# A graph convolution with sorted edges: the second stream's sums are stored as plain blocks of 127 or 255 rows, and the place columns are multiplied in bf16

## The reference, cut to what matters

```python
def _rgcn_edge_conv(h, xe, src, dst, etype, w, rt, b):
    m = jax.nn.relu(h[src] + xe)
    seg = etype * n + dst
    sums = jax.ops.segment_sum(m, seg, num_segments=R * n)
    cnt = jax.ops.segment_sum(jnp.ones((m.shape[0],), m.dtype), seg, num_segments=R * n)
    mean = sums / jnp.maximum(cnt, 1.0)[:, None]
    out = jnp.einsum('rnd,rdo->no', mean.reshape(R, n, -1), w)
    return out + h @ rt + b
...
h = jnp.maximum(_layernorm(x, axis=-1), 0.0)
for l in range(L):
    h = _rgcn_edge_conv(h, xe, src, dst, edge_type, weight[l], root[l], bias[l])
    h = _batch_norm(h, bn_gamma[l], bn_beta[l])
    if l != L - 1:
        h = jax.nn.relu(h)
return x + h
```

## Time and profile before

| | |
|---|---|
| median of 3 runs | 2361.72 us (2359.91 to 2362.99) |
| profiled execution | 2347.37 us, span 2345.3 us |
| mean granted TensorE clock | 0.912 |
| PE busy | 1950.2 us, 83% |
| PE weight load busy | 1623.0 us, 69% |
| DVE busy | 1434.1 us, 61% |
| ACT busy | 1193.5 us, 51% |
| POOL busy | 1443.9 us, 62% |

### The profile page before, as it was taken

The page is one execution under the profiler, slowest core; times in us unless marked ns, Lnnn a source line. Parts: engine busy times, 40 slices in busy tenths (PEclk is TensorE's granted clock), DMA queues, the critical chain, the costliest instruction groups (busy, mean ns, idle before and its releaser), DMA issues. The chain is left out here.

```text
span 2345.3 us, 58410 instructions
## 1 busy us (share of the span) xinstructions
PE 1950.2 (83%) x22268; PEld 1623.0 (69%) x22268; DVE 1434.1 (61%) x4328; ACT 1193.5 (51%) x2472; POOL 1443.9 (62%) x1377
## 2 busy tenths in 40 slices
PE   2499999999998889799788887787778787769866
PEld 1288888888777767799676675666556566659855
DVE  8766777777776565488765554444444444528554
ACT  0166777877776665344244443343333343424565
POOL 6746777777777775200377777777777777741000
PEclk8599999999999999899898999988998889979966
DMA  8724555555554553799633333333323333259799
GB/s 325 304 83 130 148 158 162 157 153 157 148 152 137 155 159 92 283 418 417 222 111 110 110 107 96 97 93 98 89 83 97 88 99 90 68 198 329 243 416 402
DMA packets 260695, 409.54 MB, mean 175 GB/s; under 512 B 38627, under 2 KB 170334, under 8 KB 260412
## 3 DMA queue, kind: packets, MB, share of 16 engines
q1 hardware_dynamic: 192566, 225.92, 29.2%
q0 software_dynamic: 46192, 99.84, 14.7%
q10 hardware_dynamic: 21654, 79.99, 8.4%
HBM read 255.41 MB, written 150.19 MB: 173 GB/s over the span
## 5 line engine op out<-in xcount | busy, mean ns | idle before, releaser
L853 POOL DMA_INDIRECT acc<-arena x550 | 583.9, 1062 | 223.6 <-issue 160.6
L1775 PE MATMUL ps_o<-arena 128*128 128x128 f32 x3152 | 458.9, 306 | 217.8 <-DVE arena L1224 215.2
L1775 PEld LDWEIGHTS ps_o<-arena 128*128 128x128 f32 x3152 | 420.8, 215 | 305.6 <-DVE arena L1224 298.5
L838 POOL DMA_INDIRECT arena<-h_rows,arena x394 | 438.9, 1114 | 301.0 <-DMA h_rows<-chunk_mem 181.2
L838 POOL DMA_INDIRECT arena<-in_x_dram,arena x394 | 403.4, 1024 | 125.5 <-issue 119.7
L1706 PE MATMUL ps_t<-arena 128*128 128x256 f32 x1576 | 453.2, 411 | 12.1 <-DVE arena L1198 8.1
L1198 DVE TENSOR_SCALAR arena<-arena 128x256 f32<-128x256 f32 x788 | 273.9, 410 | 128.3 <-PE ps_o L1725 128.1
L1184 DVE TENSOR_TENSOR arena<-arena,bn_b 128x512 f32<-128x512 f32 (+1 forms) x99 | 69.7, 704 | 448.7 <-DMA arena<-h_rows,arena 448.7
L1706 PEld LDWEIGHTS ps_t<-arena 128*128 128x128 f32 x1576 | 274.7, 194 | 96.2 <-issue 69.5
L1511 ACT ACTIVATE arena<-ps_o 1x512 f32<-1x512 f32 (+1 forms) x196 | 113.2, 577 | 423.7 <-PE ps_o L1775 423.6
L1480 ACT ACTIVATE arena<-ps_t 128x512 f32<-128x512 f32 x396 | 233.2, 589 | 179.7 <-PE ps_t L1706 179.5
(11 more groups left out here) (281 smaller groups left out, 2399.8 us busy)
## 6 DMA issues: line engine op xcount, KB each, us to landing
arena<-in_edge_attr_dram SPq DMA_DIRECT2D x190, 256.0 KB
chunk_mem<-acc SPq DMA_DIRECT2D x55, 512.0 KB, 8.4
acc<-arena ACTq DMA_DIRECT2D x28, 896.0 KB, 24.0
arena<-in_x_dram SPq DMA_DIRECT2D x45, 512.0 KB, 9.7
arena<-acc SPq DMA_DIRECT2D x43, 512.0 KB, 12.4
chunk_mem<-hn_rows SPq DMA_DIRECT2D x41, 512.0 KB, 12.7
out_dram<-arena ACTq DMA_DIRECT2D x38, 512.0 KB, 9.0
acc<-arena SPq DMA_DIRECT2D x238, 56.0 KB
```

Of the source, the lines that this page charges most:

```text
L838: pool.indirect_dma_start(out=hb[:, hb_slot(gg), t // NG, :], out_offset=None, in_=(x, h1_tab)[l], in_offset=at(src_t[:, t:t + 1])).then_i ...
L853: pool.indirect_dma_start(out=acc[l], out_offset=at(idx_t[:, t:t + 1]), in_=ob[:, gg % OB, t // NG, :], in_offset=None, **how).then_inc(co ...
L1775: last = te.matmul(ps_sum[:, c], sm[:, gg % SM, b, j, :], yb[:, gg % 2, b, j, :], start=b == 0, stop=b == NH - 1)
```

## The change

Four things change together.

1. **Blocks.** All of stream 1 (tiles 100 to 194) goes out as plain blocks: 127 rows for the first 31 tiles, 255 rows for the other 64. A block of 255 rows is two DMAs, 127 rows and 128 rows. The second takes sums that did not fit into one tile-high matrix: `place_at` and `sm` get a further column set (places minus 128), PE adds two matmuls to `node_sums` into the second product bank of that group, and ACT copies that bank to a fifth slot of `ob`. Stream 0 keeps its blocks of 112 rows, streams 2 and 3 are scattered. 190 tiles a layer are in `WIDE` now, 204 are scattered (275 before).
2. **Rings.** The larger `ob` entries leave room for OB = 3 groups, and `LAG` is 7. Since the further sums lie in the second product bank, `products(i, 1)` waits for `ob_ready` in place of `yb1_ready`.
3. **Place columns.** `place_column` reads the upper 16 bits of `pm` as bf16 and multiplies with two bf16 columns (high and low part of the number), in place of one fp32 column. DVE adds the two results, with one more instruction a group.
4. **Setup.** The setup on DVE gets some more small instructions for the new spans.

```diff
-    HB, XB, SM, OB = 20, 4, 2, 4
+    HB, XB, SM, OB = 20, 4, 2, 3
...
-    MT, LAG = 3, 10
+    MT, LAG = 3, 7
...
-    WROWS = 112
-    SPANS = ((1, NG - 4), (NG + 1, NG + 24))
+    SPANS = ((1, NG - 4, 112, 1), (NG + 1, NG + 31, 127, 1), (NG + 32, 2 * NG - 4, 255, 2))
...
+    def further(g):
+
+        return [t // NG for t in tiles(g) if t in WROWS and WROWS[t] >= P]
...
                     if gg > 0:
                         wait(sp, wide_out, 16 * windows(gg - 1))
+                    if t - 1 not in WIDE:
+                        sp.wait_ge(scat_out[(gg - 1) % OB], 16 * tiles_done(gg - 1, OB))
                     first = sp.value_load(first_i[0:1, t:t + 1], min_val=0, max_val=P * (F + WB * P - 1))
-                    sp.dma_start(acc[l][bass.ds(first, WROWS), :], ob[1:1 + WROWS, gg % OB, t // NG, :]).then_inc(wide_out, 16)
+                    rows = min(WROWS[t], T)
+                    sp.dma_start(acc[l][bass.ds(first, rows), :], ob[1:1 + rows, gg % OB, t // NG, :]).then_inc(wide_out, 16)
+                    if t // NG in further(g):
+                        k = H + further(g).index(t // NG)
+                        sp.dma_start(acc[l][bass.ds(first + T, P), :], ob[:, gg % OB, k, :]).then_inc(wide_out, 16)
...
-                    at = ps_side[:, 0:NH * H].rearrange("p (b j) -> p b j", b=NH)
-                    own.link(v.tensor_scalar(place_i[:, :, 0:w], at[:, :, 0:w], 0.25, None, ALU.add))
+                    at = ps_side[:, 0:2 * NH * H].rearrange("p (b j k) -> p b j k", b=NH, k=2)
+                    own.link(v.tensor_copy(place_mid[:, :, 0:w], at[:, :, 0:w, 1]))
+                    own.link(v.scalar_tensor_tensor(place_i[:, :, 0:w], at[:, :, 0:w, 0], 0.25, place_mid[:, :, 0:w], ALU.add, ALU.add))
...
+                    w += len(further(g))
...
+                n = len(further(g))
+                if n > 0:
+                    a_.activation(ob[:, gg % OB, H:H + n, :].rearrange("p w d -> p (w d)"), product_bank(gg, 1)[:, 0:n * D], ACT.Copy)
...
-                    last = te.matmul(ps_side[:, k:k + 1], pm[:, g % 2, j, b * P:(b + 1) * P], ikey_t[:, t:t + 1], start=True, stop=True)
+                    top = pm[:, g % 2, j, b * P:(b + 1) * P].bitcast(BF16)[:, 1:2 * P:2]
+                    last = te.matmul(ps_side[:, 2 * k:2 * k + 2], top, place_b[:, t, :], start=True, stop=True)
...
-                    wait(pe, (yb_ready, yb1_ready)[b], gg - 1)
+                    wait(pe, (yb_ready, ob_ready)[b], gg - 1)
...
+                    if sorted_:
+                        for k, j in enumerate(further(g)):
+                            for b in range(NH):
+                                last = te.matmul(product_bank(gg, 1)[:, k * D:(k + 1) * D], sm[:, gg % SM, b, H + k, :], yb[:, gg % 2, b, j, :],
+                                                 start=b == 0, stop=b == NH - 1)
```

More of the change, by code:

```diff
@@ L120, in tiles @@
         return [s * NG + g for s in range(H) if s * NG + g < NT]
-    WROWS = 112
-    SPANS = ((1, NG - 4), (NG + 1, NG + 24))
-    WIDE = [t for a, b in SPANS for t in range(a, b + 1)]
+    SPANS = ((1, NG - 4, 112, 1), (NG + 1, NG + 31, 127, 1), (NG + 32, 2 * NG - 4, 255, 2))
+    WIDE = [t for a, b, rows, n in SPANS for t in range(a, b + 1)]
+    WROWS = {t: rows for a, b, rows, n in SPANS for t in range(a, b + 1)}
     WB = WIDE[-1] // P + 1
-    assert all(a % NG > 0 and b % NG + 2 < NG and a // NG == b // NG for a, b in SPANS) and WROWS < P
+    FURTHER = 2
+    assert all(a % NG > 0 and b % NG + 2 < NG and a // NG == b // NG and rows < n * P for a, b, rows, n in SPANS)
+    def further(g):
+        return [t // NG for t in tiles(g) if t in WROWS and WROWS[t] >= P]
     def listed(g):
@@ L136, in windows @@
     def windows(gg):
-        return sum(len(in_window(k % NG)) for k in range(gg + 1))
+        return sum(len(in_window(k % NG)) + len(further(k % NG)) for k in range(gg + 1))
+    assert all(len(further(g)) <= FURTHER and (not further(g) or len(tiles(g)) == H) for g in range(NG))
+    assert all(further(g) == list(range(further(g)[0], further(g)[-1] + 1)) for g in range(NG) if further(g))
     ORDER = [(g, t) for g in range(NG) for t in tiles(g)]
@@ L275, in gnn_kernel @@
         assert used["mk"] <= MKW
-        src_t = early([P, NTP], U32)
-        idx_t = early([P, NTP], U32)
+        src_t = early([P, NTA], U32)
+        idx_t = early([P, NTA], U32)
         dst_t = early([P, NTP])
         ikey_t = early([P, NTP])
-        inv_t = early([P, NTP])
+        inv_t = early([P, NTA])
         xb = early([P, XB, H, D])
@@ L971, in _ @@
             own.mark(v.tensor_tensor(over[:, :], dstf[:, 0:WB, T], dstf[:, 0:WB, 0], ALU.subtract))
-            for k, (a, b) in enumerate(SPANS):
+            own.join()
+            own.link(v.tensor_scalar(width[:, :], is_wide[:, :], float(SPANS[0][2]), None, ALU.mult))
+            for k, (a, b, rows, n) in enumerate(SPANS):
                 if k > 0:
                     own.link(v.tensor_scalar(behind[:, :], t0, float(SPARE_ROW + P * a), None, ALU.is_ge))
-                    own.link(v.tensor_tensor(is_wide[:, :], is_wide[:, :], behind[:, :], ALU.add))
+                    own.mark(v.tensor_tensor(is_wide[:, :], is_wide[:, :], behind[:, :], ALU.add))
+                    own.link(v.scalar_tensor_tensor(width[:, :], behind[:, :], float(rows), width[:, :], ALU.mult, ALU.add))
                 own.link(v.tensor_scalar(behind[:, :], t0, float(SPARE_ROW + P * b), None, ALU.is_gt))
-                own.link(v.tensor_tensor(is_wide[:, :], is_wide[:, :], behind[:, :], ALU.subtract))
-            own.link(v.scalar_tensor_tensor(over[:, :], over[:, :], -float(WROWS), is_wide[:, :], ALU.add, ALU.mult))
+                own.mark(v.tensor_tensor(is_wide[:, :], is_wide[:, :], behind[:, :], ALU.subtract))
+                own.link(v.scalar_tensor_tensor(width[:, :], behind[:, :], -float(rows), width[:, :], ALU.mult, ALU.add))
+            own.link(v.tensor_tensor(over[:, :], over[:, :], is_wide[:, :], ALU.mult))
+            own.link(v.tensor_tensor(over[:, :], over[:, :], width[:, :], ALU.subtract))
             for b in range(WB):
@@ L987, in _ @@
             own.link(v.memset(behind[:, :], 1.0))
-            for a, b in SPANS:
+            for a, b, rows, n in SPANS:
                 own.link(v.scalar_tensor_tensor(behind[:, :], t0, float(SPARE_ROW + P * (b + 1)), behind[:, :],
@@ L1052, in _ @@
             spares = srcf[0:1, :, :].rearrange("p b e -> p (b e)")[:, 0:WB * P]
-            own.mark(v.tensor_scalar(spares, iota_f[0:1, 0:WB * P], float(P), float(SPARE_ROW), ALU.mult, ALU.add))
+            for b in range(WB):
+                own.mark(v.tensor_scalar(spares[:, b * P:(b + 1) * P], iota_f[0:1, 0:P], float(P), float(SPARE_ROW + b * P * P), ALU.mult, ALU.add))
             own.join()
@@ L1751, in products_any @@
                     wait(pe, yb_ready, gg - 1)
-                    wait(pe, yb1_ready, gg - 1)
+                    wait(pe, ob_ready, gg - 1)
                     for j, t in enumerate(tiles(g)):
```

43 lines of the change are left out of this document (28 added, 15 removed).

## The result

On the chip of the first comparison the changed kernel has a median of 2343.13 us (2325.19 to 2358.47, 20 runs) and the kernel before 2360.72 us (2354.60 to 2365.52, 20 runs): ratio 0.9927, 95% interval 0.9913 to 0.9941, 17.6 us less. On three further chips the kernel before had medians of 2343.5 to 2345.6 us. So the changed kernel took the same time on both of its chips, and the kernel before was slower by some 15 us on the first one; why, stays open. The two profiles of the changed kernel have spans of 2350.0 and 2340.3 us, that of before 2345.3 us. I forecast 43 us less. The first comparison has the direction and less than half of the size; the second can't be told from no change.

A forecast was written before the change was run, and what follows sets the result against it. PE bounds layer 0's early groups, POOL its later ones and all of layer 1. Layer 1 -92, layer 0 +36, ends +9, setup +4 sum to -43 us, put on the median: 2318 us, own range 2285 to 2350, overall 2225 to 2410.

The forecast's parts named there:

- what takes the place in layer 0: Layer 0: late half chunk sets 8.7 us a group (9 to 31, +17), 9.0 us (32 to 95, +20); clock +3.
- my second rival: 127-row block spread over engines or its tail hidden; layer 0 at 8.0 and 7.55 us a group; 2219 us, chance 0.12.
- Groups 1 to 8, no half chunks: Layer 0's first groups: POOL's 7.3 us and some loss, 7.4 us a group, -4 us in all.
- The chain of blocks: Both layers: 6.8 us a group, hidden in the steady part under 8.45 and 9.0 us, showing only in the last groups.
- At 1.37 to 1.41 us an instruction a group costs POOL 8.2 to 8.4 us: Layer 1, groups 25 to 95: one scatter fewer a group, period taken as 8.45 us in place of 9.8.
- the term of -92: Layer 1: 71 scatters leave POOL, 71 x (9.8 - 8.45) = 96 us gained, written as 92.
- setup +4: Setup: some 20 small instructions more on DVE cost 4 us, bounds 0 and 8.
- The ends: Last groups of each layer: block chain shows and POOL's scatter of group 96 waits, +4 to +5 us each, +9.
- The place columns: Layer 0, PE: bf16 takes 0.6 us a group in place of 1.95 us, so 1.2 us less.
- the fourth rival: Layer 1: PE with further sums, partly at 1.2 GHz, holds it at 9.2 us a group; 2367 us, chance 0.10.
- OB = 3: Ring of `ob`: 2 groups of 8 us left against a round trip of some 4 us, so no cost.
- The third rival: Block holds its engine longer than 3.5 us; at 5.2 us layer 0 +74, layer 1 and ends +14; 2406 us, chance 0.28.

The follow-up runs named there:

- the second: The changed kernel, unedited, compared again with the kernel before on another chip: 2343.28 us against 2346.13 us, ratio 0.9989.
- 1: Changed kernel with SP issuing the half chunk's load ahead of the blocks, not behind them: 2215.54 us, ratio 0.9453.
- 2: Changed kernel with each block of 127 rows issued as 112 and 15 rows, order unchanged: 2278.01 us, ratio 0.9729.
- 3: Changed kernel with the half chunk's load ahead of the blocks and 127-row blocks split into 112 and 15: 2197.91 us, ratio 0.9381.
- 4: Changed kernel with `LAG` 10 again, OB still 3: 2236.65 us, ratio 0.9545.
- 5: Kernel before with `LAG` 7 alone: 2344.71 us, ratio 1.0001.
- 8: Changed kernel with layer 1's `same_node` as eight to ten narrow instructions with one SBUF input: 2278.51 us, ratio 0.9714.
- 9: Kernel before with layer 1's `same_node` as eight instructions with one SBUF input and a scalar per row: 2291.56 us, ratio 0.9772.
- 10: Changed kernel without the fifth column set on DVE, leaving out some right sums; PE reads another set: 2325.17 us, ratio 0.9921.
- 6: Kernel before with blocks of 127 in place of 112 rows, `LAG` still 10: 2400.73 us, ratio 1.024.
- 7: Kernel before with bf16 place columns alone: 2326.22 us, ratio 0.9924.

## Why the prediction was wrong in size

**Right: what takes the place in layer 0.** From group 9 on, the half chunk's load behind `window_rows(n - 7)` and the block of 127 rows on one engine set layer 0's pace. 1, 2, 3 and 4 show it: undo the order or the `LAG` and 123 to 130 us of layer 0 come back; split the block and 60 to 64 do. 5 shows that the order was free in the kernel before. The Trainium skill, page "DMA: Bandwidth & Descriptors" (why a DMA increments its semaphore by 16, how many engines), has 1 engine for 127 rows and 16 for 112; the 7.4% and experiment 2 agree. Groups 8 to 31 cost 19 us more (forecast 17) and 31 to 95 27 and 23 us in the two profiles (forecast 20 and 3 for the clock). The load was 1.5 us longer in flight and issued 0.3 us later, where I had 2.0 us. That the 9.0 us a group came out so well (measured 9.10 and 9.05) is in part luck: my second rival gave 8.0 us for these groups with a block that is spread, and 2 measured 8.56, with one more issue in the round (its load is issued 4.41 us behind the start of `sums_out`, against 3.85 us). So the round without the block was sized too short, and the block too dear.

**Failed: "Groups 1 to 8, no half chunks ... 8 x -0.5 = -4", and "The chain of blocks is 2.35 + 1.17 + 3.3 = 6.8 us a group ... so hidden".** These groups cost 13 us more, 9.6 us each. The load of group n gates the statistics of group n, which run four groups ahead of its products, so the first half chunks reach back into these groups. And the first load was late for blocks that had to land, not for sums. ACT, SP and DVE in order of time, from `sums_out` of group 2 on:

```profile
143.43 0.57 ACT L1557 ACTIVATE arena<-ps_o 128x512 f32<-128x512 f32 x1
...
146.99 1.50 SPq L741 DMA_DIRECT2D acc<-arena  x2
...
154.55 1.42 SPq L741 DMA_DIRECT2D acc<-arena  x2
156.02 0.86 SPq L759 DMA_DIRECT2D spare<-in_x_dram  x1
...
162.26 0.87 DVE L1180 BATCH_NORM_STATS2 st<-spare 128x6 f32<-128x128 f32 x4 [13.52 <-DMA spare<-in_x_dram]
```

and SP's waits between 130 and 165 us:

```profile
SPq L738 <- DMA acc<-arena: 20.3, 1, 20.3
SPq L21 <- DMA acc<-arena: 8.6, 2, 4.4
```

The sums of group 2 were out at 144.0 us, its blocks left at 154.55. Group 1's had waited for the scatters of group 0 (L738, a wait that came with the change), those of group 2 for group 1's to land, and the load stood behind them. From one group's blocks to the next it is 7.6 and 8.6 us (154.55, then 163.12), above the 6.8 us that I had hidden. Before, this load was issued at 135.54 us with no block ahead of it. In 2 (blocks split) groups 0 to 8 took 8.50 us each, in 1 (load first) 7.82, in 4 (`LAG` 10) 6.96, against 9.63. These groups are 17 of the 20 us by which layer 0 was under-forecast. What the wait at L738 costs by itself was not tested.

**Failed: "At 1.37 to 1.41 us an instruction a group costs POOL 8.2 to 8.4 us. I take 8.45".** Layer 1's groups 24 to 95 ran at 8.77 and 8.66 us, because an instruction costs 644.7 / 435 = 1.48 us. Step by step the term of -92 lacks 35 us: 15 to 23 us for that; 9 us since 9.8 us was too high for before (its groups 24 to 95 took 686.3 us, 9.67 each); 10 to 12 us because groups 0 to 24, which I took as unchanged, became slower; and the 4 us that I had taken off go the other way. I named the right cause (the fifth column set of L1224) and sized it from the difference of two means, 1.37 and 1.41, which says nothing of it: over whole groups POOL's mean before is 1.109 us in groups 0 to 24 and 1.105 us in 24 to 95. It could have been read in order of time. POOL before, at 1502 us, and DVE's L1224 beside it:

```profile
1500.97 1.04 POOL L838 DMA_INDIRECT arena<-h_rows,arena  x1 [0.30 <-issue]
1502.32 1.52 POOL L838 DMA_INDIRECT arena<-h_rows,arena  x1 [0.31 <-issue]
1504.15 0.99 POOL L853 DMA_INDIRECT acc<-arena  x1 [0.30 <-issue]
...
1501.74 1.28 DVE L1224 TENSOR_TENSOR arena<-arena 128x512 f32<-128x512 f32 x2
```

Against 8 the stretch now is 5.96 x (1.179 - 1.036) = 0.85 us a group, before it was 0.64 (9). 8 and 9 show the contention, and 10 what the fifth set adds: without it groups 24 to 95 ran at 8.42 us, close to my 8.45, which is 17 to 25 us of these 71 groups.

In groups 0 to 24 POOL is full before and now. It did 143 and 145 instructions in that stretch in place of 138, at 1.125 and 1.126 us in place of 1.109, each with 0.30 us behind it: 9 and 12 us more, the whole difference. The blocks of 127 rows have a part in it: in 6, where they alone came in, these groups took 7.9 us more and POOL's mean was 1.167 us, and in 2, with the blocks split, they took 199.2 us, 5 and 7.5 us less than in the changed kernel. Why more instructions fall into this stretch is not shown.

**Failed: setup +4.** The start is 4.6 us shorter, not longer, and 4.0 us of that come with the bf16 place columns alone (7). I had counted instructions on DVE, not what the first group waits for.

**Right, or too small to matter.** The ends cost 5 us, not 9. The place columns take 0.35 us (forecast 0.6); 7 sizes the whole edit at 17.6 us where POOL sets the later groups. In layer 1 POOL sits idle for 2.3 us beyond its issue gaps, so the fourth rival (PE holds layer 1) is out. OB = 3 does make ACT wait for landed blocks there, as the waits of 1500 to 2045 us show, behind a POOL that is full:

```profile
ACT arena L1556 <- DMA acc<-arena: 69.2, 34, 4.6
```

The third rival (a block longer than 3.5 us) is out as well: 2.9 us.

**The level.** I put the sum on 2361.7 us, the median of the runs, which the 20 runs on the first chip repeat, while four other chips gave 2343.5 to 2346.1 us. By the parts the change is worth 0 us (-4.6 + 56 + 2 - 57 + 3.4), by the two comparisons 17.6 and 2.9 us less. How much a change this small is worth depends here on the chip.

## What to carry to other kernels

The blocks of 127 rows went through one engine here and held what queued behind them: cut 127 into 112 and 15 (65 us), and put a load that an engine will soon wait for ahead of stores that can be late (128 us, for an exchange of two statements). When an engine is full, price its instructions in order of time, beside what the neighbour does, and not by means over stretches: the 1.52 among the 1.0 us was worth 54 us in the kernel before. When a change shortens a lag, follow the late load to the first group that it gates, not to the group in which it is issued, and follow its own queue back to what it really waits for there.

## What the runs showed of the hardware

In layer 1's groups 24 to 95 POOL's indirect DMAs took 1.52 us in the median mostly beside a pair of DVE `tensor_tensor` with both inputs in SBUF (1.28 us for the two) and 1.78 us beside a pair of 1.55 us; they took 0.97 and 0.98 us on average beside no DVE instruction, and 1.01 to 1.04 us over all once `same_node` reads one SBUF tensor and a column (8, 9). The Trainium skill, page "SBUF — State Buffer" (who interferes with whom), has a DVE instruction with two SBUF inputs contend with GpSimd instructions that read SBUF, and takes descriptor generation to be spared by `tensor_tensor`, an inference by its own words. The rows agree with the first; an indirect DMA on POOL isn't spared. Behind one block of 127 rows an issue took 0.73 us in the median, behind two in a row 2.9 to 3.9 us. And the kernel before differed by 15 us between chips, while the changed one had the same time on its two.
